# Transposes of g set in front of bf16 products, in a mixture-of-experts kernel on one core

## The reference

```python
x = x + tanh(g_xattn[0]) * xattn(layernorm(x), ctx, ctx, Wq, Wk, Wv)
x = x + tanh(g_ffn[0]) * ffn(layernorm(x), ...)

def ffn(x):                                   # 2048 tokens, D = 256, HID = 512
    gates = normalized top-2 of softmax(x @ Wg.T)
    h1 = x @ W1[e].T + low-rank part + b1[e]  # for each expert e
    h3 = x @ W3[e].T + low-rank part + b3[e]
    g  = silu(h1) * h3
    y  = sum over e of gates[:, e] * (g @ W2[e].T + low-rank part + b2[e])
```

## Time and profile before

| what | us |
|---|---|
| timed executions | 330.58, 328.56, 330.31 |
| their median | 330.31 |
| span of the profiled execution, first to last instruction | 325.4 |
| median less that span | 4.9 |
| PE busy within the span | 297.9 (92%) |

### The profile page before, as it was taken

How to read it: one execution, slowest core, us unless ns; L and a number is a source line. 1 busy time by engine, 2 the same in 40 slices (tenths; PEclk the granted TensorE clock), 3 DMA queues, 4 the chain that set the end, 5 groups by cost and what they waited for, 6 DMA issues and landing times. The chain is left out here.

```text
span 325.4 us, 7435 instructions
## 1 busy us (share of the span) xinstructions
PE 297.9 (92%) x1755; PEld 230.0 (71%) x1755; DVE 248.2 (76%) x607; ACT 206.0 (63%) x486; POOL 210.8 (65%) x246
## 2 busy tenths in 40 slices
PE   7589989999997798999999999999999999999960
PEld 3468778788886656776777777777777777777740
DVE  2679879889999998697988976767776776777750
ACT  5635755766878577787675565665675665675550
POOL 2457878888893098866756656766577776666241
PEclk9799999999999699999999999999999999999996
DMA  7968997999972169567747675766533223333100
GB/s 265 391 158 240 280 297 253 294 279 278 278 244 85 17 225 296 138 201 200 205 139 206 175 187 186 175 187 197 148 56 55 52 51 66 53 45 61 20 0 0
DMA packets 30424, 54.35 MB, mean 167 GB/s; under 512 B 7232, under 2 KB 15808, under 8 KB 30112
## 3 DMA queue, kind: packets, MB, share of 16 engines
q1 hardware_dynamic: 14672, 36.10, 34.1%
q0 software_dynamic: 7488, 9.36, 16.7%
q10 hardware_dynamic: 8224, 8.42, 8.6%
HBM read 41.92 MB, written 10.65 MB: 162 GB/s over the span
## 5 line engine op out<-in xcount | busy, mean ns | idle before, releaser
L1079 POOL DMA_INDIRECT out<-ys,cols x39 | 64.7, 1660 | 58.4 <-DMA out<-ys,cols 33.0
L883 ACT ACTIVATE gh<-bank 128x512 fp32r<-128x512 f32 x39 | 23.4, 599 | 61.0 <-PE bank L648 61.0
L640 PE MATMUL bank<-WH,xh 128*128 x156 | 55.7, 438 | 0.1
L1056 POOL DMA_INDIRECT xg<-xn_rows,colg x39 | 40.0, 1026 | 20.5 <-POOL colg L1034 10.3
L992 POOL TENSOR_TENSOR WL<-stage,WH 128x512 bf16<-128x512 f32 x38 | 47.9, 1278 | 7.3 <-ACT WH L752 7.1
L640 PE MATMUL bank<-WH,xl 128*128 x156 | 49.0, 395 | 0.0
L640 PE MATMUL bank<-WL,xb 128*128 x156 | 47.2, 385 | 0.0
L752 ACT ACTIVATE WH<-stage 128x512 fp32r<-128x512 f32 x38 | 22.9, 628 | 17.7 <-DVE stage L1110 14.5
L640 PEld LDWEIGHTS bank<-WH,xl 128*128 128x128 f32 x156 | 29.2, 188 | 6.8 <-DVE xl L1493 0.4
L1497 DVE TENSOR_TENSOR gl<-bank,gh 128x512 fp32r<-128x512 f32 x39 | 26.9, 689 | 8.8 <-ACT gh L883 8.7
L657 PE MATMUL bank<-WH,gh 128*128 x156 | 32.0, 327 | 1.5 <-ACT gh L883 1.5
(11 more groups left out here) (229 smaller groups left out, 702.2 us busy)
## 6 DMA issues: line engine op xcount, KB each, us to landing
BB<-biases_in SPq DMA_DIRECT2D x16, 640.0 KB, 4.1
stage<-w_all_in SPq DMA_DIRECT2D x38, 256.0 KB, 5.1
BA<-biases_in SPq DMA_DIRECT2D x8, 640.0 KB, 3.9
WL<-w_all_in SPq DMA_DIRECT2D x10, 256.0 KB, 4.7
LS<-WH SPq DMA_DIRECT2D x45, 48.0 KB
xn_rows<-xn ACTq DMA_DIRECT2D x8, 256.0 KB, 4.1
out<-x ACTq DMA_DIRECT2D x7, 256.0 KB, 3.1
cx<-ctxT_in ACTq DMA_DIRECT2D x6, 256.0 KB, 6.5
```

Source lines behind the costliest of these rows:

```text
L640: last = nc.tensor.matmul(dst[:, :], lhs[p][:, c * P:(c + 1) * P], W[:, bass.ds(e * (UNITS * UC) + (2 * kind + c) * UC, HID)], start=(part ...
L883: nc.scalar.activation(gh[:], pG[:, :], ACT.Copy).then_inc(s_gh, 1)
L1056: nc.gpsimd.indirect_dma_start(out=xg[q][:], out_offset=None, in_=xn2_d[0:JA * P, :] if i < NA else xn2_d, in_offset=bass.IndirectOffsetOn ...
L1079: nc.gpsimd.indirect_dma_start(out=out_rows, out_offset=bass.IndirectOffsetOnAxis(ap=cols[:, i:i + 1], axis=0), in_=ys[p][:], in_offset=No ...
```

## The change

On PE alone, the four transposes of g and the bf16 products of a tile change places. Two transposes now stand in h1, each in front of one of its two `xb` products, and two in h3, whose `xb` products come first instead of last. The transposes of x, between h1 and h3 before, now stand between the `xb` and the `xh` products of h3. The last tile's transposes of g, behind the loop, stay together. No other engine's instructions change, and no instruction is added or removed on PE.

```diff
-            def g_transposes(i):
-                pe.wait_ge(s_g, i + 1)
-                for c in range(HC):
-                    last = nc.tensor.transpose(pG[:, c * P:(c + 1) * P], g[:, c * P:(c + 1) * P], ident[:])
-                last.then_inc(s_gT, 1)
+            def g_transpose(c):
+                return nc.tensor.transpose(pG[:, c * P:(c + 1) * P], g[:, c * P:(c + 1) * P], ident[:])
...
             def tile(i, q, first, more):
                 p = q % 2
-                up(pH1, i, p, expert(q), 0, s_h1)
+                e = expert(q)
+                pos_wait(pe, s_h1b, i)
+                pe.wait_ge(s_xh, i + 1)
+                for c in range(CH):
+                    up(pH1, p, e, 0, xh, WH, c, start=(c == 0))
+                pe.wait_ge(s_xl, i + 1)
+                for c in range(CH):
+                    up(pH1, p, e, 0, xl, WH, c)
+                pe.wait_ge(s_xb, i + 1)
                 if not first:
-                    g_transposes(i - 1)
-                if more:
-                    x_transposes(i + 1, (q + 1) % XBUF)
+                    pe.wait_ge(s_g, i)
+                for c in range(CH):
+                    if not first:
+                        g_transpose(c)
+                    last = up(pH1, p, e, 0, xb, WL, c, stop=(c == CH - 1))
+                last.then_inc(s_h1, 1)
                 if first:
                     pe.wait_ge(s_wl, (E - 2) * UNITS + 4)
-                up(pH3, i, p, expert(q), 1, s_h3)
+                pos_wait(pe, s_h3b, i)
+                for c in range(CH):
+                    if not first:
+                        g_last = g_transpose(CH + c)
+                        if c == CH - 1:
+                            g_last.then_inc(s_gT, 1)
+                    up(pH3, p, e, 1, xb, WL, c, start=(c == 0))
+                if more:
+                    x_transposes(i + 1, (i + 1) % XBUF)
+                for c in range(CH):
+                    up(pH3, p, e, 1, xh, WH, c)
+                for c in range(CH):
+                    last = up(pH3, p, e, 1, xl, WH, c, stop=(c == CH - 1))
+                last.then_inc(s_h3, 1)
```

More of the change, by code:

```diff
@@ L631, in x_transposes @@
                 last.then_inc(s_xT, 1)
[L633 to L643, removed]
@@ L645, in g_transposes, with up @@
-            def g_transposes(i):
-                pe.wait_ge(s_g, i + 1)
-                for c in range(HC):
-                    last = nc.tensor.transpose(pG[:, c * P:(c + 1) * P], g[:, c * P:(c + 1) * P], ident[:])
-                last.then_inc(s_gT, 1)
[L651 to L655, removed]
-                    for c in range(HC):
-                        last = nc.tensor.matmul(pY[:, 0:D], lhs[:, c * P:(c + 1) * P],
-                                                W[:, bass.ds(e * (UNITS * UC) + 4 * UC + c * D, D)],
-                                                start=(part == 0 and c == 0), stop=(part == 2 and c == HC - 1))
+            def up(dst, p, e, kind, lhs, W, c, start=False, stop=False):
+                return nc.tensor.matmul(dst[:, :], lhs[p][:, c * P:(c + 1) * P],
+                                        W[:, bass.ds(e * (UNITS * UC) + (2 * kind + c) * UC, HID)], start=start, stop=stop)
@@ new lines, in g_transpose, with down, y_tile @@
+            def g_transpose(c):
+                return nc.tensor.transpose(pG[:, c * P:(c + 1) * P], g[:, c * P:(c + 1) * P], ident[:])
+            def down(e, lhs, W, c, start=False, stop=False):
+                return nc.tensor.matmul(pY[:, 0:D], lhs[:, c * P:(c + 1) * P],
+                                        W[:, bass.ds(e * (UNITS * UC) + 4 * UC + c * D, D)], start=start, stop=stop)
+            def y_tile(i, e):
+                pos_wait(pe, s_ys, i)
+                pe.wait_ge(s_gh, i + 1)
+                for c in range(HC):
+                    down(e, gh, WH, c, start=(c == 0))
+                pe.wait_ge(s_gl, i + 1)
+                for c in range(HC):
+                    down(e, gl, WH, c)
+                pe.wait_ge(s_gb, i + 1)
+                for c in range(HC):
+                    last = down(e, gb, WL, c, stop=(c == HC - 1))
@@ L687, in tile @@
                         pe.wait_ge(s_wl, (E - 1) * UNITS)
-                    down(i - 1, expert((q - 1) % XBUF))
+                    y_tile(i - 1, expert((q - 1) % XBUF))
                 if i == 0:
@@ L718, in _ @@
             tile_steps(pe, tile)
-            g_transposes(NT_SLOTS - 1)
-            down(NT_SLOTS - 1, expert((NT_SLOTS - 1) % XBUF))
+            pe.wait_ge(s_g, NT_SLOTS)
+            for c in range(HC):
+                last_gT = g_transpose(c)
+            last_gT.then_inc(s_gT, 1)
+            y_tile(NT_SLOTS - 1, expert((NT_SLOTS - 1) % XBUF))
         @block.scalar
```

## The result

The changed kernel took 334.81 us (median of ten runs, 331.72 to 336.99); the kernel before, run beside it, 330.66 us (median of ten, 328.56 to 332.24). The ratio is 1.012, with a 95% interval of 1.008 to 1.016. The forecast was 335.6 us, with a range of 332.0 to 337.6.

What follows compares the result with a forecast made beforehand. PE's work and an equally long loop through ACT (4.80 us a tile) bound the kernel; losses of 3.6 + 1.6 + 0.1 = 5.3 us on a 325.4 us span give 330.7, plus 4.9 makes 335.6 us, range 332.0 to 337.6.

Steps and rivals of the forecast that it cites:

- The bounds of before: In a steady tile before the change, PE's own work and a loop through ACT both take 4.80 us.
- the loop: Tile start to last transpose of g, ACT to gb's end, sequencer to next xh: 4.80 us, becoming 5.01.
- the chain's 1% "issue": Profile page: 1% of the chain that ended last is "issue", read as PE's work alone binding the kernel.
- The price of the last transpose: Last transpose of g starts 0.21 us later in the tile, costing 0.20 us in each tile the loop sets.
- The sequencer's part: PE's register instructions wait for gb, so the next xh load comes 0.85 us after gb's end, unchanged.
- The rival that it isn't the bound: PE's queue gets ahead of the wait for gb, PE's work decides: 329.2 us, not slower; chance 0.18.
- PE's saving of 0.03 us a tile: bf16 loads behind transposes instead of fp32r products save PE 0.03 us a tile, at most 1.2 us in 38 tiles.
- Exposed loads: Rival: each bf16 load behind a transpose costs about 0.1 us, so 0.5 us a tile, 344 us; chance 0.03.
- Which tiles: Loss by stretch: tiles 0 to 5 nothing, 6 to 19 1.6 us, 20 to 37 3.6 us, last tile 0.1 us.
- The wait for g: PE's wait moves to 1.03 us into a tile; g comes at about 0.5, half a microsecond ahead, costing nothing.
- what would show it: Expected signs: steady tile 5.0 us, idle loads 0.25 us, pairs 0.33 us, scatters waiting less for one another, more for ys.
- the 4.9 us between span and median: Fixed addition from the profiled span to the median of runs, taking the forecast span of 330.7 to 335.6 us.

Runs made afterwards that it cites:

- E6: The kernel before, with ACT making gb ahead of the small gate operation instead of behind it; 329.84 us, ratio 1.003 to the kernel before.
- E7: The kernel before, with gb's products always reading the first expert's low weights, so needing no register instructions; 332.3 us (one run), steady tile 4.81 us.
- E3: The changed kernel without alternation: one bf16 product of h3 ahead of all four transposes of g, kept together; 334.43 us, ratio 1.016 to the kernel before.
- E4: The changed kernel with the last transpose of g behind h3's second bf16 product instead of in front; 340.30 us, ratio 1.036 to the kernel before.
- E1: The changed kernel, with ACT making gb ahead of the small gate operation, PE's order kept; 331.28 us, ratio 1.006 to the kernel before.
- E2: The changed kernel with gb's products always reading expert 0's low weights, so without register instructions; 327.91 us, ratio 0.998 to the kernel before.
- E5: The changed kernel with all four transposes of g ahead of h1's bf16 products; 332.33 us, ratio 1.008 to the kernel before, steady tile 4.94 us.
- E8: E5 with the transposes of x moved right behind those of g; 332.61 us, ratio 1.014 to the kernel before, steady tile 4.79 us.
- E9: E5 with ACT making gb right behind gh, ahead of the copies of x and the gate; 331.26 us, ratio 1.010 to the kernel before.
- E11: E9 with a plain scatter that writes instead of adding; 325.06 us, ratio 0.984 to the kernel before.
- E10: The changed kernel with ACT making gb right behind gh, ahead of the copies of x and the gate; 340.30 us, ratio 1.040 to the kernel before.

## Why the prediction was right

- **The bounds of before.** Shown by E6 and E7: PE's work is 4.81 us, the loop as long. The prediction took its first hint from the chain's 1% "issue", and there it read too much: those are shares of the span, and that chain was followed over its last 132 us only. The rows of tile 24 and of the end of tile 19, on which the loop rests, bear it without the chain.
- **The price of the last transpose.** Its place is the cause: E3 has the price without the alternation, E4 doubles it, E1 takes it away from ACT's side. It was 0.20 us by the forecast and is 5.005 - 4.826 = 0.18 by the medians of the steady tiles. That is the 3.3 instead of 3.6 us in tiles 20 to 37.
- **The sequencer's part.** 0.84 us, as forecast, and 35 idle times put down to "issue". The rival that it isn't the bound falls with E2. That none of the register instructions starts before the end of `gb` was read rightly; the reason given, that the wait stands on the first of them, is not needed, since in E2 it stands on a product and holds the sequencer all the same.
- **PE's saving of 0.03 us a tile.** E7 against E2: 0.026. The Trainium skill's rule that the queue pulls a weight load ahead of a product in flight (TensorE: Matmul & The Clock Gate, "What happens when you issue a matmul") would have made it nothing; these two runs show that a bf16 load behind an fp32r product was not wholly hidden (0.227 us to the next product), and behind a transpose is (0.216, as between the fillers of the earlier trace rows).
- **Exposed loads.** A pair takes 0.32 to 0.33 us; E3, where the four transposes stand together, has the same tile. This rival falls.
- **Which tiles.** 1.6 us in tiles 6 to 19 as forecast, by waits for scatters that ended sooner: tiles 16 and 19 lost theirs (5.00 and 5.01 us, before 5.21 and 5.27). Tiles 0 to 5 paid 0.2, not nothing; the last tile paid nothing, not 0.1. This rests on one profile of each kernel, and ahead of tile 20 profiles differ by more than that: E6 and E7, with steady tiles as before, took 73.1 and 71.8 us for tiles 6 to 19. So the agreement in tiles 6 to 19 may be in part luck; that of tiles 20 to 37 is not.
- **The wait for g.** It stood 0.6 us ahead of need in steady tiles. In tiles 1 and 12 PE waited there, which the forecast didn't price: all transposes of g waited 1.4 us for `g` in the whole execution (0.3 before).
- **What was wrong in "what would show it".** The scatters did not wait less for one another: 41.4 us in 25 waits, before 33.0 in 22. Only ACT's waits for them went. That they would wait more for `ys` held: 16.6 us in 10 waits, before 13.8 in 7. And the prediction spoke of one loop through ACT where there are two, which lie 0.06 us apart in the changed kernel; it cost nothing there, and 0.15 us a tile in E5, where I had forgotten it.
- **The size as a whole.** The tile stage lost 5.1 us in the profile against 5.3 forecast; the medians lie 4.15 apart. In the later runs an execution's time is 1.8 us over its span, so of the 4.9 us between span and median that the forecast took as fixed, some 3 us were that profiled execution of before being a quick one. For the sum it made no difference. Why the medians lie a microsecond closer than the tile stages of the two profiles stays open.

What stays open: E8's median is 4.1 us over before's. Its profile shows 2.3 us of that in the tile stage, above all in tiles 1, 16 and 17, where E6 lost as much; that the timed runs lost the rest in the same way, or that E8's order is the cause, was not shown. Nor was a third buffer for `ys` tried, which might let scatters fall behind without stopping ACT.

## What to carry over

An engine that shows 92% busy and no gap can still have a loop through another engine beside it that is exactly as long, and the page's chain does not name that loop: add up the steps of the loop from one tile, and compare the sum with the engine's own work, before moving anything that starts the loop. Where such a loop sets the tile, not the cost but the place of a transpose in it counts, one for one (0.21 us later, 0.18 to 0.22 us more), and everything in that engine's queue ahead of the result counts with it. A shorter steady tile is worth little in the stretch where another chain, here the scatters, goes no faster.

## What the runs showed of the hardware

- Register instructions of PE's sequencer that stand behind a wait cost time after the wait even when PE has work to do, about 0.12 us each: without four of them the next tile's first register instruction came 0.26 us after the end of `gb` instead of 0.74 (E2), of which 0.20 us showed in the tile before PE's own products set it. The sequencer's `MOVE` behind the wait came 0.06 us after the end of `gb`, though there the wait stood on a product.
- A scatter that adds holds POOL 1.60 us and a plain one 1.01 (E9, E11). On average of a profile, from the scatter of tile 24 on, the adding one lands 3.5 to 3.6 us after its start and the plain one 2.4 to 2.6; from tile 2 to tile 19 both need about 1 to 2 us more (4.6 to 5.1, and 4.3 to 4.7). The loads of weights and biases run there (the core's DMA engines are busy 67% of the time from 151 to 220 us before, 39% from 220 to 307); that they are the cause was not tested.
- Whatever PE's steady tile was, 4.78 to 5.23 us, the adding scatters of tiles 2 to 20 started 5.0 to 5.3 us apart in all twelve kernels that have them, most of them 0.27 us behind the landing of the one before; where the tile was longest, in E4 and E10, about a third came later than that.
